# An expert feed-forward kernel: block 0 in plain fp32, and branches with the ninth block's end in line

## The reference

```python
h = gelu(x @ Wi[e] + bi[e])                # 256 -> 1024, exact gelu
o = h @ Wo[e] + bo[e]                      # 1024 -> 256
r = o + x
mu = mean(r); var = mean(square(r - mu))
y = (r - mu) * rsqrt(var + 1e-12) * gamma[e] + beta[e]
```

## Time and profile before

| | |
|---|---|
| median of 3 runs | 131.44 us (130.99 to 132.53) |
| profiled execution, whole time | 131.33 us |
| its span, first to last instruction | 129.4 us |
| TensorE (PE) busy | 114.2 us, 88% of the span |
| VectorE, ScalarE, GpSimd busy | 100.3, 96.2, 69.3 us |
| chain that ended last | PE 64%, DVE 14%, issue 7%, DMA 6%, ACT 3% |
| granted TensorE clock, mean | 0.967 of full |

### The profile page before, as it was taken

The page is one execution under the profiler, slowest core; times in us unless marked ns, Lnnn a source line. Parts: engine busy times, 40 slices in busy tenths (PEclk is TensorE's granted clock), DMA queues, the critical chain, the costliest instruction groups (busy, mean ns, idle before and its releaser), DMA issues.

```text
span 129.4 us, 2750 instructions
## 1 busy us (share of the span) xinstructions
PE 114.2 (88%) x880; PEld 110.6 (85%) x880; DVE 100.3 (78%) x191; ACT 96.2 (74%) x186; POOL 69.3 (54%) x84
## 2 busy tenths in 40 slices
PE   6979960999999999999999999999999996968910
PEld 6758851999999999999999999999999996957900
DVE  3500569959899999989998998999899658946370
ACT  3104399999999899989989998998999638860100
POOL 4041048138298749839883983888398417202220
PEclk9976998599999999999999999999999999999997
DMA  2889999999479939966992997599582210110111
GB/s 72 285 182 372 394 329 401 387 392 372 174 213 403 356 90 363 390 225 196 398 382 72 318 388 271 183 400 352 130 314 77 68 46 3 41 45 5 46 41 41
DMA packets 21144, 29.81 MB, mean 230 GB/s; under 512 B 2112, under 2 KB 11328, under 8 KB 21120
## 3 DMA queue, kind: packets, MB, share of 16 engines
q1 hardware_dynamic: 18208, 23.84, 54.1%
q10 hardware_dynamic: 2048, 3.35, 8.2%
q0 software_dynamic: 864, 2.36, 4.8%
HBM read 27.18 MB, written 2.36 MB: 228 GB/s over the span
## 4 chain that ended last, share of the span: by engine, by line
PE 64%; DVE 14%; issue 7%; DMA 6%; ACT 3%; SPq 2%; POOL 1%; DVEq 0%; POOLq 0%
PE sums_ps L758 12%; PE sums_ps L708 11%; PE sums_ps L707 11%; PE preact L734 9%; PE preact L708 9%; PE preact L707 9%; DMA xT_in<-x_columns 6%; DVE wo_r L590 4%; DVE h_lo L602 3%; DVE wi_lo L584 3%; PE preact L685 2%; DVE r L609 2%; SPq L246 2%; DVE centred L615 1%; POOL rstd L376 1%
## 5 line engine op out<-in xcount | busy, mean ns | idle before, releaser
L758 PE MATMUL sums_ps<-wo_r,h_lo 128*128 128x256 f32 x144 | 41.5, 288 | 6.0 <-DVE wo_r L590 4.5
L708 PE MATMUL sums_ps<-wo_r,h_hi 128*128 128x256 f32 x144 | 41.1, 286 | 0.1
L707 PE MATMUL sums_ps<-wo_r,h_hi 128*128 128x256 f32 x144 | 41.1, 285 | 0.0
L734 PE MATMUL preact<-xT_r,wi_lo 128*128 128x256 f32 x128 | 36.4, 284 | 0.4 <-DVE xT_r L595 0.4
L707 PE MATMUL preact<-xT_r,wi_hi 128*128 128x256 f32 x128 | 36.1, 282 | 0.0
L708 PE MATMUL preact<-xT_r,wi_hi 128*128 128x256 f32 x128 | 36.0, 281 | 0.0
L758 PEld LDWEIGHTS sums_ps<-wo_r,h_lo 128*128 128x128 f32 x144 | 27.6, 192 | 6.7 <-issue 5.2
L468 ACT ACTIVATE preact<-preact,params 128x256 f32<-128x256 f32 x64 | 25.8, 441 | 3.1 <-PE preact L708 3.0
L708 PEld LDWEIGHTS sums_ps<-wo_r,h_hi 128*128 128x128 f32 x144 | 27.7, 192 | 0.3 <-issue 0.3
L707 PEld LDWEIGHTS sums_ps<-wo_r,h_hi 128*128 128x128 f32 x144 | 27.6, 192 | 0.0
L258 POOL DMA_INDIRECT xs<-x_rows,row_of x18 | 21.1, 1175 | 9.2 <-issue 9.1
(11 more groups left out here) (67 smaller groups left out, 109.7 us busy)
## 6 DMA issues: line engine op xcount, KB each, us to landing
wo_in<-w_out SPq DMA_DIRECT2D x8, 1024.0 KB
wi_in<-w_in SPq DMA_DIRECT2D x7, 1024.0 KB, 8.5
params<-vectors SPq DMA_DIRECT2D x9, 388.0 KB, 6.8
y_rows<-xs SPq DMA_DIRECT2D x35, 64.0 KB, 2.2
xT_in<-x_columns SPq DMA_DIRECT2D x34, 64.0 KB, 5.9
wi_in<-w_in ACTq DMA_DIRECT2D x4, 512.0 KB, 5.3
wo_in<-w_out ACTq DMA_DIRECT2D x2, 512.0 KB, 8.9
xs<-x_rows,row_of POOLq DMA_INDIRECT x18, 5.8
```

What stands on the lines that cost most here:

```text
L707: nc.tensor.matmul(columns, weight, parts[:, 0, :], start=False, stop=False)
L708: return nc.tensor.matmul(columns, weight, parts[:, 1, :], start=False, stop=stop)
L734: nc.tensor.matmul(columns, wi_lo[:, t % 2, c, k, :], xT_r[:, t % 2, k, 0, :], start=(k == 0), stop=False)
L758: nc.tensor.matmul(columns, h_lo[:, t % 2, c, tokens], wo_r[:, t % 2, c, 0, :], start=(c == 0), stop=False)
```

## The change

Block 0 splits nothing. Its GELU writes a new SBUF tile `h_first`, and S(0) multiplies it by the loaded `wo_in` in plain fp32. TensorE runs F(0), S(0), F(1), and then F(2,q), S(1,q) and so on. ScalarE's start is four GELUs, wi_high(1,0), x_high(1), wi_high(1,1); VectorE's is wi_low(1,0), x_low(1), wi_low(1,1). W_out 0 is loaded ahead of W_in 1, and SP waits for W_out 0's second half where it waited for W_in 1's. TensorE reads `n` behind F(1), and its last warm-up is two matmuls, not one. From the ninth block on the branches ask `n < t + 1` (`n < t + 2`) first, with the end in line and the later blocks in the `Else`; the branch for the ninth block itself stays.

```diff
-    WARM_UP = (5, 4, 1)
+    WARM_UP = (5, 4, 2)
+        h_first = sb("h_first", [P, IC, N])
...
         def from_block(eng, n, t, iteration, end):
             if t == MAX_BLOCKS:
                 end(t)
-                return
-            with eng.If(n > t):
-                iteration(t, t + 1)
-                from_block(eng, n, t + 1, iteration, end)
-                eng.nop()
-            with eng.Else():
-                end(t)
-                eng.nop()
+            elif t == MIN_BLOCKS:
+                with eng.If(n > t):
+                    iteration(t, t + 1)
+                    from_block(eng, n, t + 1, iteration, end)
+                    eng.nop()
+                with eng.Else():
+                    end(t)
+                    eng.nop()
+            else:
+                with eng.If(n < t + 1):
+                    end(t)
+                    eng.nop()
+                with eng.Else():
+                    iteration(t, t + 1)
+                    from_block(eng, n, t + 1, iteration, end)
+                    eng.nop()
...
-            sp.wait_ge(first_wi_loaded[1][1], 16)
+            sp.wait_ge(first_wo_loaded[1], 16)
...
             load_xT(act, 0, (2, 3))
-            load_first_wi(1)
             for i, (a, z) in enumerate([(0, IC // 2), (IC // 2, IC)]):
                 act.dma_start(wo_in[:, 0, a:z, :].rearrange("p c h -> p (c h)"), wo[0, :, a * H:z * H],
                               max_dma_last_dim=PIECE).then_inc(first_wo_loaded[i], 16)
+            load_first_wi(1)
...
-                    to = pre if q < NS else h_raw[:, t % 2, c - SPLIT_CHUNKS, :]
+                    to = h_first[:, c, :] if t == 0 else pre if q < NS else h_raw[:, t % 2, c - SPLIT_CHUNKS, :]
...
-            for t in range(MIN_BLOCKS - 1):
+            for q in range(BANKS):
+                gelu(0, q)
+            wi_high(1, 0)
+            x_high(1)
+            wi_high(1, 1)
+            for t in range(1, MIN_BLOCKS - 1):
                 iteration(t, True)
...
-            for t in range(MIN_BLOCKS - 1):
+            wi_low(1, 0)
+            x_low(1)
+            wi_low(1, 1)
+            for t in range(1, MIN_BLOCKS - 1):
                 iteration(t, True)
...
-            pe.wait_ge(table_ready, 1)
-            n = entry(pe, T_BLOCKS, MAX_BLOCKS, MIN_BLOCKS)
             warm_up(WARM_UP[2])
...
+                    if t == 0:
+                        last = nc.tensor.matmul(columns, h_first[:, c, tokens], wo_in[:, 0, c, :], start=(c == 0),
+                                                stop=(c == IC - 1))
+                        continue
...
-            for t in range(MIN_BLOCKS):
+            for q in range(BANKS):
+                first_product(0, q)
+            for part in range(4):
+                second_product(0, part)
+            for q in range(BANKS):
+                first_product(1, q)
+            pe.wait_ge(table_ready, 1)
+            n = entry(pe, T_BLOCKS, MAX_BLOCKS, MIN_BLOCKS)
+            for t in range(2, MIN_BLOCKS):
                 iteration(t, True)
```

More of the change, by code:

```diff
@@ L222, in load_wo @@
         def load_wo(eng, t, e):
-            if t >= WO_RING:
+            if t > WO_RING:
                 for piece in range(2):
-                    eng.wait_ge(wo_lo_done[piece], t - WO_RING + 1)
-                if RAW_BANKS:
-                    eng.wait_ge(sums_part, 4 * (t - WO_RING) + 4)
+                    eng.wait_ge(wo_lo_done[piece], t - WO_RING)
+            if t == WO_RING or t > WO_RING and RAW_BANKS:
+                eng.wait_ge(sums_part, 4 * (t - WO_RING) + 4)
             eng.dma_start(wo_in[:, t % WO_RING, :, :].rearrange("p c h -> p (c h)"),
@@ L285, in with_next @@
                 end(t + 1)
[L286 to L294, removed]
+            elif t + 1 == MIN_BLOCKS:
+                with eng.If(n > t + 1):
+                    iteration(t, True)
+                    with_next(eng, n, t + 1, iteration, end)
+                    eng.nop()
+                with eng.Else():
+                    iteration(t, False)
+                    end(t + 1)
+                    eng.nop()
+            else:
+                with eng.If(n < t + 2):
+                    iteration(t, False)
+                    end(t + 1)
+                    eng.nop()
+                with eng.Else():
+                    iteration(t, True)
+                    with_next(eng, n, t + 1, iteration, end)
+                    eng.nop()
         @block.sync
@@ L444, in wo_high @@
                 a, b = WO_PIECES[piece]
[L445 to L449, removed]
+                act.wait_ge(wo_loaded[t % WO_RING], loads_of(t, WO_RING) - (16 if t % WO_RING == 0 else 0))
                 if t >= 2:
@@ L488, in iteration @@
             def iteration(t, has_next):
-                if t == 0:
-                    gelu(t, 0)
                 if has_next:
@@ L494, in iteration @@
                     deviations(t - 2, 1)
-                if t > 0:
-                    gelu(t, 0)
+                gelu(t, 0)
                 h_high(t, 0)
@@ L499, in iteration @@
                     x_high(t + 1)
-                if t > 0:
-                    wo_high(t, 0)
+                wo_high(t, 0)
                 gelu(t, 1)
@@ L509, in iteration @@
                 h_high(t, 2)
-                wo_high(t, 0 if t == 0 else 1)
+                wo_high(t, 1)
                 gelu(t, 3)
                 h_high(t, 3)
-                if t == 0:
-                    wo_high(t, 1)
             def end(t):
@@ L599, in h_low @@
                     return
-                dve.wait_ge(h_hi_done, NS * t + q + 1)
+                dve.wait_ge(h_hi_done, NS * (t - 1) + q + 1)
                 hi, lo = (x[:, t % 2, 2 * q:2 * q + 2, :].rearrange("p c n -> p (c n)") for x in (h_hi, h_lo))
@@ L644, in iteration @@
                     centre(t - 2, 1)
-                if t >= 1:
+                if t >= 2:
                     h_low(t - 1, 3)
@@ L661, in iteration @@
                     wi_low(t + 1, 1)
[L662 to L666, removed]
+                if has:
                     wo_low(t, 0)
@@ L716, in first_product @@
                 if t >= 1:
-                    if q < NS:
-                        pe.wait_ge(h_lo_done, NS * (t - 1) + q + 1)
+                    if q < NS and t >= 2:
+                        pe.wait_ge(h_lo_done, NS * (t - 2) + q + 1)
                     else:
@@ L746, in second_product @@
                     if c % 2 == 0 and tile == 0:
-                        if c < SPLIT_CHUNKS:
-                            pe.wait_ge(h_lo_done, NS * t + c // 2 + 1)
+                        if c < SPLIT_CHUNKS and t >= 1:
+                            pe.wait_ge(h_lo_done, NS * (t - 1) + c // 2 + 1)
                         else:
@@ L751, in second_product @@
                     for piece, (first, _) in enumerate(WO_PIECES):
-                        if c == first and tile == 0:
-                            pe.wait_ge(wo_lo_done[piece], t + 1)
+                        if c == first and tile == 0 and t == 0:
+                            pe.wait_ge(first_wo_loaded[piece], 16)
+                        elif c == first and tile == 0:
+                            pe.wait_ge(wo_lo_done[piece], t)
+                    if t == 0:
+                        last = nc.tensor.matmul(columns, h_first[:, c, tokens], wo_in[:, 0, c, :], start=(c == 0),
+                                                stop=(c == IC - 1))
+                        continue
                     if c >= SPLIT_CHUNKS:
@@ L764, in iteration @@
                     first_product(t, q)
-                    if t >= 1:
-                        second_product(t - 1, q)
+                    second_product(t - 1, q)
             def end(t):
```

2 lines of the change are left out of this document (1 added, 1 removed).

## The result

The changed kernel takes 133.09 us (median of 4 runs, 132.70 to 133.82), the kernel before 131.22 (4 runs, 130.72 to 132.53): 1.6% slower, ratio 1.016 [1.009, 1.024], with the 95% interval in brackets. The forecast was 131.4, no change. The profiled execution took 133.1 us, its span 131.0 where before's was 129.4.

The account below looks back on a forecast made before the run. TensorE, fed without a gap from 33.76 us, bounds the kernel; only work before that or behind the last full iteration counts. 131.33 - 1.5 - 1.2 + 2.7 = 131.3, 131.4 as median; own range 130.6 to 132.3, for all 128.5 to 133.6.

Parts of the forecast that it names:

- the exit, +2.7: At the kernel's end, SP jumps over the code of blocks 10 to 15 with nothing covering it: 2.7 us lost.
- rival 2: SP's exit jump is dear, 5.0 us again or two shorter stalls: 133.6 us, slower than before; chance 0.13.
- "4.0": At SP's exit, the stall in us (2.7 + 1.3) beyond which the dear exit jump decides the outcome.
- The first part, -1.5: At the start, block 0 in plain fp32 lets block 1's second product proceed earlier: gain 1.5 us, ends 0.5 to 2.6.
- "Then VectorE": In the head, h_low(1,3) takes 0.60 and wo_low(1,1) 1.22 us: 34.6 + 0.60 + 1.22 = 36.4.
- Rivals 3 and 4: Block 0: TensorE warm, 130.4 us, chance 0.13; or new idle slows the clock or W_in 2 is late, 132.4 us, 0.12.
- Rival 3: TensorE is warm for block 0's first product, so gelu(1,0) can start 1.0 us earlier: 130.4 us; chance 0.13.
- The second part's gain, -1.2: At the end of block 7, the new branch sides remove VectorE's stall and TensorE's wait behind it: gain 1.2 us.
- The chance for "slower", 0.20: For the whole kernel, a measurably slower result: the dear exit jump plus a tail of the slow-clock or late-load case; chance 0.20.
- Idle VectorE gone: Sign at the end: VectorE's idle time behind its branch, L609 "issue", disappears.
- F(1) at 23.5: Sign in the head: block 1's first product starts on TensorE at 23.5 us.
- Idle 2.2 and 0.9 at S(1,0) and S(1,1): Sign in the head: TensorE idles near 2.2 and 0.9 us before the first two parts of block 1's second product.

Follow-up runs that it names:

- e7: The changed kernel with code for at most ten blocks instead of fifteen: 129.03 us, ratio 0.987 to the kernel before.
- e6: The changed kernel with SP given the new branch sides at block 8 too, so its exit is one landing: 131.50 us, ratio 1.005 to the kernel before.
- e1: The changed kernel with the old branch sides on all five engines, leaving only block 0's part: 130.74 us, ratio 0.987 to the kernel before.
- e4: The changed kernel with VectorE's finish(0,0) moved behind wo_low(1,1): 133.58 us, ratio 1.009 to the kernel before.
- e3: The changed kernel with the new branch sides on VectorE and TensorE only, old ones elsewhere: 129.13 us, ratio 0.979 to the kernel before.
- e2: The kernel before with the new branch sides alone, block 0 unchanged: 134.72 us, ratio 1.017 to the kernel before.

## Why the prediction was wrong

**The term that failed is the exit, +2.7.** Its mechanism stood as predicted: the code of the tenth to fifteenth block lies in front of the exit, SP jumps over it last with nothing covering it, and the jump stalls (e7: shorten the code and it does not). One landing was priced right, 2.5 us in the changed kernel and 2.7 in e6 against 2.8. The reason given for 2.8 did not hold as read: the DMA queues were not empty in VectorE's stall (101.9 to 104.8: share 0.19, 50 GB/s), as they nearly were at the exit (0.04 and less); they were only emptier than in SP's 5.0 us (0.70, 221 GB/s). But the landing was counted once. The text had named the second hop in rival 2, over `end(8)`, and gave that rival only 0.13. It costs 2.1 us, and e6 takes it away. In before the second hop cost 0.4 (128.7 to 129.1 on SP in the profile of before), and I carried that price over. But there two short hops led out; here the second comes right behind a far landing. The exit's rise is 3.97, against 2.7: 1.3 us of the miss. It lies at the "4.0" from which on, the prediction said, rival 2 decides. Of its two forms the shorter stalls came, not SP's 5.0 again.

**The first part, -1.5, was too large in the traces.** Profile against profile it gave 0.78, by e1's median 1.0; e1's ratio, 1.8 with a wide interval, does not exclude 1.5. The path drawn was F(1), gelu(1,0), ScalarE's 9.44 us, h_low, wo_low. ScalarE took 9.33 us for it (24.25 to 33.58), as predicted. What was missing is what stands in front of h_low(1,3) on VectorE: finish(0,0), behind rstd of GpSimd, behind residual(1) and params 0. The text held that SP's queue keeps its time, and so GpSimd's line did not move and became the wait. The failed step is "Then VectorE": it lets h_low(1,3) start at 34.6, 0.1 behind h_high(1,3). The rows already spoke against it. In before h_high(1,3) ended at 33.97 and h_low(1,3) started at 35.10, 1.13 later, which cost nothing as TensorE came to S(1,1) only at 38.05. With h_low(1,3) left at 35.10, S(1,1) could start at 35.10 + 0.60 + 1.22 + 0.15 = 37.07, a gain of 0.98. In e1, whose F(0) had the slow clock as assumed, ScalarE kept the forecast exactly (gelu(1,0) 17.23 us behind F(0)'s start, as 25.1 - 7.87), and VectorE started h_low(1,3) 0.56 behind it; the gain from F(0) to S(1,1) was 1.14.

Rivals 3 and 4 met in the profiled execution: F(0) at full clock (7.17 us), and the clock falling at the new pause. W_in 2 landed near 23.29, in time by rival 4's 24.1, but it ended a wait of 4.72 us. Rival 3 took 23.11 for the landing, though wi_high(2,0) started then without a wait; its gain of 1.0 did not come, as the fast F(0) moved ScalarE and not GpSimd's line. The fallen clock cost S(1,1) nothing here (0.49 us of wait is left behind it); e4 shows it as the next to hold.

**The second part's gain, -1.2, was right and a little small.** The stall of VectorE went and S(7,1) has no wait; wo_low(8,1) starts at 114.99 instead of 117.02, so 2.03 - 0.78 = 1.25 came from there. The whole stretch gave 1.62, and e3's median is 1.6 under e1's. 0.25 of the other 0.37 is a gap in S(8,1) of before, where one matmul starts at 119.30 and the next at 119.67 (0.12 apart elsewhere), which the changed kernel has not; its cause was not tested.

**Sum.** Forecast -1.5 - 1.2 + 2.7 = 0; measured in the profile -0.78 - 1.62 + 3.97 = +1.57. The head lost 0.7 and the exit 1.3 more, the middle gave 0.4 back. 133.09 lay outside the forecast's own 130.6 to 132.3 and inside the range for all, 128.5 to 133.6. The chance for "slower", 0.20, rested on a second hop that should have been priced nearly like the first.

**What it said would show it.** Idle VectorE gone, yes. F(1) at 23.5: 21.40, since F(0) was fast. Idle 2.2 and 0.9 at S(1,0) and S(1,1): 3.23 and 0.49 there, 2.07 and 1.00 in e1, whose F(0) had the slow clock as assumed. S(1,1) at 36.6, with F(0) at 7.87: 37.18. Drain 3 us behind the last branch: 4.6, with the second hop's branch between. Last stores 2.7 earlier: the wait for them ended 2.35 earlier.

The section that the prediction weighed, in the Trainium skill, "Runtime: NRT & Kernel Launch", "Instruction fetch mechanics", says that an engine stalls when it branches to instructions it does not hold. The trace agrees on SP: instruction packets are all that moves in its two stalls, and in e7, with less code to jump over, neither packets nor stalls are left. The section gives no price; in the changed kernel it is 2.1 to 3.4 us each on SP, VectorE, ScalarE and TensorE. GpSimd's 0.5 us does not fit it without a further reason. How many instructions an engine holds no run here shows.

## What to carry to other kernels

Choose which side of a branch lies in line engine by engine, not once for all: the engine that feeds the critical path wants the likely case in line, the engine that leaves last (here SP, behind the last stores) wants its exit close by. e3 did just this and took 2.1% off where the uniform layout added 1.6%. Count the landings on the way out one by one, each at nearly the full price, and when a wait is taken off one chain, follow every operation that stands ahead in the consumer's own order (here finish(0,0)), and what in the load queue hangs on it if you move it (e4).

## What was not expected of the hardware

- A far jump out of the last block cost SP 2.5 us (2.7 in e6) with the DMA engines all but idle (share 0.04), and VectorE 3.1, ScalarE 2.8 and TensorE 3.35 with the last stores still moving (0.22, 0.22 and 0.11). GpSimd went the same way in 0.5 us; why it is spared was not tested. The branches of the changed kernel on GpSimd, VectorE and ScalarE:

```profile
L306 POOLq COMPARE_BRANCH  x1: 38/38/38, 122.3 to 122.3; - x1
L306 DVEq COMPARE_BRANCH  x1: 51/51/51, 123.2 to 123.2; - x1
L306 ACTq COMPARE_BRANCH  x1: 38/38/38, 124.4 to 124.4; - x1
L297 POOLq COMPARE_BRANCH  x1: 38/38/38, 122.8 to 122.8; - x1
L297 DVEq COMPARE_BRANCH  x1: 41/41/41, 126.3 to 126.3; - x1
L297 ACTq COMPARE_BRANCH  x1: 38/38/38, 127.2 to 127.2; - x1
```

- The short hop over `end(8)` cost SP 2.1 us in the changed kernel and 2.2 in e2, right behind a landing, and 0.2 in e7, where the jump in front of it was short.
- The granted clock of TensorE fell to 0.50 behind the pause at S(1,0) in the changed kernel, though the engine had been busy without a gap from 7.67 to 28.86. In e2 it did not fall behind a pause of 3.50 us.
